# The choice by eleven rounds of three bits, gathers a stage ahead and new order lists in a gated-attention and expert kernel

## The chip, the cores and the metric

The kernel runs on one core of one Trainium2 chip. The metric is device time in microseconds (us), the median of repeated runs. One more execution was recorded by the hardware profiler; its rows are what the prediction reads. The engines are TensorE (PE in the rows, PEld for its weight loads), VectorE (DVE), ScalarE (ACT), GpSimd (POOL) and SyncE (SP), which only issues transfers.

## What is computed

Four batches of 512 tokens with 512 features go through a gated cross-attention and then a gated mixture of experts. Cut to what matters:

```python
kv   = ctx @ W_k.T + b_k                          # 4 x 512 x 128
sim  = (layernorm(x) @ kv) @ kv.T * scale         # per batch, 512 x 512
attn = softmax(normalised(sim) * gamma + beta)
x    = x + tanh(g_xattn) * attn
h    = layernorm(x)                               # 2048 tokens
shared = ffn(h, shared_w1, shared_w2)             # x1 * silu(x2) @ w2
aff  = sigmoid(h @ gate_w + bias)                 # 7 experts
mask = top 2 experts of each token
sel[e] = the 292 tokens with the largest affinity among those that chose e
routed[sel[e]] += ffn(h[sel[e]], w1[e], w2[e]) * aff
out  = x + tanh(g_ffn) * (shared + routed)
```

The 292nd largest affinity of each expert must be found exactly, and ties are filled in token order.

## The kernel before, in words

It is written by hand: each engine has one list of calls, and semaphores order them between engines. An engine works strictly in its list's order, so where a call stands decides what it can hold up.

*Front.* For batch b TensorE transposes the context (`context`), projects keys (`keys`), transposes x (`x_cols`, four columns) and the centred keys (`keys_back`), multiplies (`attend`, `scores`). ScalarE copies each result out of PSUM (`context_copy`, `x_copy`, `keys_copy`, `keys_back_copy`, `out_copy`) and sums squares (`squares`, `exps`, `row_squares`). VectorE computes row statistics of x (`x_stats`), centres keys, scales scores by an inverse root that GpSimd computes (`score_variance`, `scale_scores`), adds the attention (`add_attention`) and normalises rows (`row_variance`, a root on GpSimd, `row_normal`). The rows are transposed again (`rows_back`) and split into two parts of reduced precision: ScalarE makes the upper (`rows_upper`), VectorE the lower (`rows_lower`); each product is three matmuls over such parts. Weights are split the same way (`upper_*`, `lower_w1`, `lower_w2`).

*Shared expert and gate.* `gate` and `logits` make the seven scores of each token, `take_logits` stores them. `up(f, half, part)` is 12 matmuls of 512 columns, `down(f, t)` 6. Between them `gate_tanh`, `gate_first`, `gate_second`, `gate_upper` and `gate_lower` form the hidden values. A down tile is added to x in two ways: tiles below `EARLY` = 10 are scaled by ScalarE (`shared_rows`) and added to the output in DRAM by accumulating transfers that GpSimd issues (`add_to_out`), while x itself was stored before; the rest are added by VectorE (`add_shared`) and stored by SP (`store_sums`).

*Choice.* `choose_two` (from L1320, its first operation is the sign shift) marks each token's two experts and turns scores into ordered integers, cut into four byte planes masked by the choice (L1332). Eight rounds then find each expert's threshold, four bits at a time: `compare(r)` compares all scores of a plane with 15 candidates (four operations of 7 x 15 x 4 = 420 elements, L1353), `count(r)` sums them over partitions on TensorE (four matmuls of 420 columns, L451), `take_digit(r)` (L1358 to L1363) turns the sums into the next digit. Shared products stand between the counts on TensorE and gate steps between the rounds on VectorE. Then `flag`, `total_and_prefix`, `slots_of_chosen`, `place_told`, `hot_slots`, `slot_products` and `token_rows` give each expert's list of token rows `tok`.

*Routed experts.* GpSimd gathers 292 rows for an expert in three indirect transfers (`gather`, L1158) and adds its results to the output by three scattering ones (L1183). TensorE transposes the gathered rows of the next expert (`gathered`) inside the current expert's products; the first matmuls of an expert are on L712. Gathered rows lie in two buffers, so the gather of expert e + 2 waits until e's rows are transposed and its weights copied; in GpSimd's list it stands just ahead of the scatter of expert e, and behind that of e - 1.

The few lines of the choice that carry the size of a round:

```python
LEVELS, NIBBLE = 4, 16
CAND = NIBBLE - 1
ROUNDS = 2 * LEVELS
for q in range(NB):   # compare
    v.tensor_tensor(hit[:, q, :, :, :], bc(scores[:, :, ts].unsqueeze(2), [P, E, CAND, TT]),
                    bc(thresholds[:, :, :].unsqueeze(1), [P, E, CAND, TT]), ALU.is_ge)
```

## Time and profile before

| | |
|---|---|
| median of 3 runs | 260.25 us (259.28 to 262.13) |
| profiled execution | 259.54 us |
| its span | 257.8 us |
| granted TensorE clock, mean | 0.973 |
| busy share PE, DVE, ACT, POOL | 89%, 71%, 54%, 32% |
| bytes moved | 38.19 MB, mean 148 GB/s |

The page cuts the span into 40 slices of 6.4 us and prints each engine's busy share in tenths, the clock that TensorE was granted and the transfers' load:

```profile
PE   2998968999999988999999996999979999999920
PEld 1745533677568766677668775978868989898810
DVE  0486989789979898888988999858473848482300
ACT  3447995797794854221334304565745666664320
POOL 6502002003021020100112257315757858553370
PEclk9999995999999999999999999999999999999995
DMA  6899000800436023910750939994979988370651
```

Slices 1 to 16 are the front, 17 to 23 the choice, 25 to 38 the seven routed experts. An instruction's duration in the rows includes the time in the pipeline, so two of one kind start closer together than one lasts.

### The profile page before, as it was taken

The numbers are of one execution on the slowest core, as the hardware profiler recorded it, in microseconds if no ns is written. First come the engines' busy times: TensorE is split into PE (matmuls) and PEld (weight loads), VectorE is DVE, ScalarE is ACT, GpSimd is POOL, SyncE is SP. The second block draws the span as 40 slices with busy tenths as digits, with TensorE's granted clock in tenths as the row PEclk, the third lists the DMA queues.
The fourth block names the chain that finished last, engine by engine and source line by source line (L and its number), as shares of the span: only waits on it lengthen the run. The fifth ranks groups of instructions, "written<-read, shape, count | busy, mean of one in ns | idle before, by whom it ended". The sixth has DMA issues, their size and how long they took to land.

```text
span 257.8 us, 3584 instructions
## 1 busy us (share of the span) xinstructions
PE 228.6 (89%) x1182; PEld 173.4 (67%) x1182; DVE 183.9 (71%) x458; ACT 138.9 (54%) x314; POOL 82.8 (32%) x88
## 2 busy tenths in 40 slices
PE   2998968999999988999999996999979999999920
PEld 1745533677568766677668775978868989898810
DVE  0486989789979898888988999858473848482300
ACT  3447995797794854221334304565745666664320
POOL 6502002003021020100112257315757858553370
PEclk9999995999999999999999999999999999999995
DMA  6899000800436023910750939994979988370651
GB/s 208 279 350 317 5 0 17 309 0 0 185 143 245 0 93 119 385 57 3 89 74 12 165 82 335 233 377 98 238 213 226 249 280 161 96 95 5 89 68 25
DMA packets 23084, 38.19 MB, mean 148 GB/s; under 512 B 4054, under 2 KB 6262, under 8 KB 23066
## 3 DMA queue, kind: packets, MB, share of 16 engines
q1 hardware_dynamic: 16570, 25.30, 28.5%
q0 software_dynamic: 5536, 11.62, 25.3%
q10 hardware_dynamic: 960, 1.05, 1.2%
q8 instruction: 9, 0.15, 0.2%
q14 instruction: 9, 0.07, 0.1%
HBM read 22.70 MB, written 15.26 MB: 147 GB/s over the span
## 4 chain that ended last, share of the span: by engine, by line
PE 40%; DVE 21%; ACT 12%; issue 11%; DMA 7%; POOL 4%; DVEq 2%; POOLq 1%; ACTq 0%
PE bank L375 22%; PE bank L370 6%; PE bank L408 4%; DMA out<-yr,tok_out 3%; DMA xg_tail<-h_rows,tok 2%; ACT junk L849 2%; POOL out L1183 2%; DVEq L1194 2%; DVE hit L1353 2%; DVE prob L1228 2%; DVE prob L1222 2%; ACT yr L1032 2%; DVE xs L1239 2%; PE bank L451 1%; PE bank L426 1%
## 5 line engine op out<-in xcount | busy, mean ns | idle before, releaser
L1183 POOL DMA_INDIRECT out<-yr,tok_out x21 | 34.2, 1629 | 31.6 <-ACT yr L1032 16.4
L784 ACT ACTIVATE gT_hi<-gf 128x292 fp32r<-128x292 f32 (+3 forms) x23 | 11.4, 500 | 30.2 <-DVE gf L1275 18.0
L375 PE MATMUL bank<-hT_hi,w1s_hi 128*128 128x512 f32 x64 | 26.7, 417 | 0.3 <-DVE th L1270 0.3
L375 PE MATMUL bank<-hT_hi,w1s_lo 128*128 128x512 f32 x64 | 25.1, 392 | 0.0
L375 PE MATMUL bank<-hT_lo,w1s_hi 128*128 128x512 f32 x64 | 25.0, 390 | 0.0
L1032 ACT ACTIVATE yr<-bank,wslot 128x512 f32<-128x512 f32 (+1 forms) x21 | 13.9, 687 | 13.5 <-PE bank L375 12.6
L375 PE MATMUL bank<-w2s_hi,gT_hi 128*128 128x512 f32 (+1 forms) x50 | 20.8, 415 | 0.0
L375 PE MATMUL bank<-w2s_hi,gT_lo 128*128 128x512 f32 (+1 forms) x50 | 19.6, 392 | 0.0
L375 PE MATMUL bank<-w2s_lo,gT_hi 128*128 128x512 f32 (+1 forms) x50 | 19.5, 391 | 0.0
L1158 POOL DMA_INDIRECT xg<-h_rows,tok x14 | 15.6, 1114 | 12.2 <-issue 7.7
L1109 POOL TENSOR_TENSOR rs<-vs,mhalf 128x4 f32<-128x4 f32 x4 | 4.5, 1114 | 45.1 <-DVE vs L1215 45.1
L408 PE MATMUL bank<-xT,kvc 128*128 128x512 f32 x32 | 17.5, 699 | 1.6 <-ACT xT L784 1.3
L1291 DVE TENSOR_TENSOR w1r_lo<-w_raw,w1r_hi 128x512 fp32r<-128x512 f32 x16 | 10.8, 690 | 10.5 <-ACT w1r_hi L784 10.2
L784 ACT ACTIVATE hgT_hi<-bank 128x292 fp32r<-128x292 f32 x28 | 10.5, 408 | 13.0 <-PE bank L370 12.0
L1291 DVE TENSOR_TENSOR w1s_lo<-w_raw,w1s_hi 128x512 fp32r<-128x512 f32 x16 | 10.6, 687 | 7.4 <-ACT w1s_hi L784 7.2
L1128 POOL DMA_DIRECT2D out<-xs x5 | 6.3, 1266 | 29.3 <-ACT xs L875 29.3
L414 PE MATMUL bank<-kvcT,outT 128*128 128x512 f32 x32 | 14.6, 598 | 0.3 <-ACT outT L784 0.3
L375 PE MATMUL bank<-hgT_hi,w1r_hi 128*128 128x292 f32 x48 | 14.5, 303 | 0.0
L375 PE MATMUL bank<-hgT_hi,w1r_lo 128*128 128x292 f32 x48 | 14.3, 297 | 0.0
L375 PE MATMUL bank<-hgT_lo,w1r_hi 128*128 128x292 f32 x48 | 14.2, 297 | 0.0
L375 PEld LDWEIGHTS bank<-hT_hi,w1s_hi 128*128 128x128 f32 x64 | 12.1, 189 | 3.1 <-DVE th L1270 0.7
L375 PEld LDWEIGHTS bank<-hT_hi,w1s_lo 128*128 128x128 f32 x64 | 12.0, 188 | 2.7
(221 smaller groups left out, 641.4 us busy)
## 6 DMA issues: line engine op xcount, KB each, us to landing
w_raw<-in_L_ffn_routed_w SPq DMA_DIRECT2D x7, 1024.0 KB
w_raw<-in_L_ffn_routed_w SPq DMA_DIRECT2D x7, 512.0 KB
xs<-in_x SPq DMA_DIRECT2D x3, 1024.0 KB, 12.1
h_rows<-h SPq DMA_DIRECT2D x3, 1024.0 KB, 4.2
out<-xs POOLq DMA_DIRECT2D x5, 512.0 KB
out<-xs SPq DMA_DIRECT2D x2, 1024.0 KB, 6.8
out<-xs SPq DMA_DIRECT2D x4, 512.0 KB, 5.5
ctxb<-in_ctx SPq DMA_DIRECT2D x4, 256.0 KB, 6.8
```

The lines of the kernel that those rows point to most:

```text
L370: return nc.tensor.transpose(out_ap, in_ap, ident[0:n, 0:n])
L375: last = nc.tensor.matmul(out_ap, w, m, start=first and n == 0, stop=final and n == len(todo) - 1)
L408: last = nc.tensor.matmul(front_bank(b, ATTEND)[:, :], kvc[:, j, :], xT[:, j, :], start=j == 0, stop=j == TT - 1)
L414: nc.tensor.matmul(bank[t][:, :], outT[:, t * P:(t + 1) * P], kvcT[:, :], start=True, stop=True).then_inc(p_S, 1)
L784: return nc.scalar.activation(dst, src, ACT.Copy)
L849: nc.scalar.activation(junk[:, t, :], tile_of(at), ACT.Square, bias=nmean[:, at:at + 1], accum_out=ssx[:, at:at + 1]).then_inc(e_ssx, 1)
L1032: nc.scalar.activation(yr[e % 2][0:GSZ[g], g, :], down_bank(e, g)[0:GSZ[g], :], ACT.Copy, scale=w).then_inc(f_y, 1)
L1128: g_.dma_start(out_rows[f, :, 2 * half:2 * half + 2, :], xs[:, at:at + 2, :], accum_op=ALU.add).then_inc(st_y, 16)
L1158: g_.indirect_dma_start(gathered_rows(e, g)[0:GSZ[g], 0:HW], None, h_dram, index(tok, e, g), bounds_check=T).then_inc(gath[e % 2][g], 16)
L1183: g_.indirect_dma_start(rows, index(tok_out, e, g), yr[e % 2][0:GSZ[g], g, :], None, bounds_check=T - 1, compute_op=ALU.add).then_inc(scat ...
L1194: return v.drain()
L1291: v.tensor_tensor(w[1][:, k, :], raw[:, k, :], w[0][:, k, :].bitcast(F32), ALU.subtract).then_inc(w1_lo, 1)
```

## The change

The choice takes digits of three bits: each score's ordered integer is read in six levels of six bits (`LEVELS`), cut out by shift and mask (`level_bits`) when a level begins, each level in two rounds, but one round for the last two bits. That makes eleven rounds. A round has 7 candidates, and a comparison covers half of the tokens: two operations of 7 x 7 x 8 = 392 elements, and four count matmuls of 196 columns. The upper part of a number is masked by `keep` instead of a product with `mask`.

`EARLY` goes from 10 to 14: tiles (2, 2) to (3, 1) are also scaled by ScalarE and added by accumulating transfers, two `add_to_out` more and two `store_sums` fewer, and `add_to_out(1, 1)` moves behind the first two gathers. `down(3, 3)` moves behind the first gathered transposes, its `add_shared` behind the first `gathered_lower`. The gather of expert e + 3 stands ahead of the scatter of expert e. Seven matmuls on a zeroed tile open TensorE's list. Loads of x and shared weights are issued in another order, `slots_ps` lies in bank 3, the banks of the front are assigned anew, and the lists of TensorE, ScalarE and VectorE for front and choice are written anew. The core of the diff:

```diff
-LEVELS = 4
-NIBBLE = 16
-CAND = NIBBLE - 1
-ROUNDS = 2 * LEVELS
-EARLY = 10
+BITS = 6
+LEVELS = -(-32 // BITS)
+DIGIT = 8
+CAND = DIGIT - 1
+HT = NT // 2
+ROUNDS = 2 * LEVELS - 1
+WARM = 7
+EARLY = 14
...
             load_x(1)
-            load_x(2)
-            load_raw(0, sw1[0], sw2[0])
             sp.wait_ge(p_ctxT, 1)
             load_ctx(2)
+            load_x(2)
             load_x(3)
+            sp.wait_ge(p_ctxT, 2)
+            load_ctx(3)
+            load_raw(0, sw1[0], sw2[0])
...
-                    pe.wait_ge(r_hit, NB * r + q + 1)
-                    last = nc.tensor.matmul(counts, ones[:, :], hit[:, q, :, :, :].rearrange("p e c t -> p (e c t)"),
+                    if q % 2 == 0:
+                        pe.wait_ge(r_hit, 2 * r + q // 2 + 1)
+                    last = nc.tensor.matmul(counts, ones[:, :], hit[:, q // 2, :, :, q % 2 * TT:q % 2 * TT + TT].rearrange("p e c t -> p (e c) t"),
                                             start=q == 0, stop=q == NB - 1)
...
+            pe.wait_ge(c_warm, 1)
+            for _ in range(WARM):
+                nc.tensor.matmul(bank[0][:, :], junk[:, 0, 0:P], junk[:, 0, :], start=True, stop=True)
             pe.wait_ge(c_pool, 2)
-            context(0)
             pe.wait_ge(ld_wk, 16)
             transpose(bank[7][:, 0:C], Wk_rows[:, :]).then_inc(c_wk, 1)
...
             pe.wait_ge(c_start, 3)
@@ -617,56 +626,56 @@
             pe.wait_ge(e_hT, 14)
             up(2, 1, 0)
             count(1)
-            down(0, 1)
             pe.wait_ge(e_hT, 15)
-            down(0, 2)
+            up(2, 1, 1)
             count(2)
             pe.wait_ge(e_hT, 16)
+            down(0, 2)
+            count(3)
+            pe.wait_ge(e_y, 1)
+            up(3, 0, 0)
+            count(4)
+            pe.wait_ge(e_y, 2)
             down(0, 3)
+            count(5)
             pe.wait_ge(e_u, 5)
             down(1, 0)
-            count(3)
-            pe.wait_ge(e_y, 1)
-            up(2, 1, 1)
-            count(4)
             pe.wait_ge(e_g, 5)
-            up(3, 0, 0)
-            count(5)
+            down(1, 1)
+            count(6)
             pe.wait_ge(e_u, 6)
-            down(1, 1)
-            pe.wait_ge(e_y, 2)
             down(1, 2)
-            count(6)
+            count(7)
+            pe.wait_ge(e_g, 6)
+            up(3, 0, 1)
+            count(8)
             pe.wait_ge(e_y, 3)
-            up(3, 0, 1)
-            count(7)
+            down(1, 3)
+            count(9)
+            pe.wait_ge(e_u, 7)
+            up(3, 1, 0)
+            count(10)
             pe.wait_ge(e_y, 4)
-            down(1, 3)
-            pe.wait_ge(e_y, 5)
             down(2, 0)
             pe.wait_ge(c_start, 4)
             total_and_prefix()
-            pe.wait_ge(e_g, 6)
+            pe.wait_ge(e_y, 5)
             down(2, 1)
-            pe.wait_ge(e_u, 7)
-            up(3, 1, 0)
             pe.wait_ge(e_y, 6)
+            down(2, 2)
+            pe.wait_ge(e_y, 7)
             up(3, 1, 1)
-            pe.wait_ge(e_y, 7)
+            pe.wait_ge(e_g, 7)
+            down(2, 3)
+            pe.wait_ge(e_y, 8)
             slot_products(0)
-            pe.wait_ge(e_g, 7)
-            down(2, 2)
             slot_products(1)
-            pe.wait_ge(e_y, 8)
-            down(2, 3)
+            pe.wait_ge(e_u, 8)
+            down(3, 0)
             pe.wait_ge(e_y, 9)
-            down(3, 0)
+            down(3, 1)
             pe.wait_ge(e_y, 10)
-            down(3, 1)
-            pe.wait_ge(e_u, 8)
...
+            pe.wait_ge(e_y, 11)
+            pe.wait_ge(e_g, 8)
+            pe.wait_ge(e_y, 12)
+            pe.wait_ge(r_idx, 1)
             gathered_first()
+            down(3, 3)
+
...
             gather(0)
             gather(1)
+            add_to_out(1, 1)
             add_to_out(2, 0)
+            add_to_out(2, 1)
+            add_to_out(3, 0)
+            def gather_into_free(e):
+                pool.wait_ge(q_hgT, KD * (e - 1))
+                pool.wait_ge(f_w, e - 1)
+                gather(e)
+
+            gather_into_free(2)
             for e in range(E):
-                if e + 2 < E:
-
-                    pool.wait_ge(q_hgT, KD * e + KD)
-                    pool.wait_ge(f_w, e + 1)
-                    gather(e + 2)
+                if e + 3 < E:
+                    gather_into_free(e + 3)
...
+                v.scalar_tensor_tensor(keep[:, :, :], one[:, 0, :, :], -1.0, one[:, 1, :, :], ALU.mult, ALU.subtract).then_inc(r_one, 1)
+                settle()
+                v.tensor_tensor(ordered[:, :, :], ordered[:, :, :], keep[:, :, :], ALU.bitwise_and)
+                settle()
+                level_bits(0)
+                settle()
+                v.tensor_copy(top[:, :, :], bits[:, :, :])
+                settle()
+
+            def level_bits(level):
+                low_bit = max(32 - BITS * (level + 1), 0)
+                width = 32 - BITS * level - low_bit
+                v.tensor_scalar(bits[:, :, :], ordered[:, :, :], low_bit, 2 ** width - 1, ALU.logical_shift_right, ALU.bitwise_and)
+
+            def high_digit(r):
+                return r % 2 == 0 and r < ROUNDS - 1
 
             def compare(r):
                 level = r // 2
-                scores, thresholds = rest, low if r % 2 else high
+                scores, thresholds = rest, high if high_digit(r) else low
                 if r % 2:
-                    above = plane[:, LEVELS - 1, :, :] if level == 0 else rest[:, :, :]
+                    above = top[:, :, :] if level == 0 else rest[:, :, :]
                     v.tensor_tensor(rest[:, :, :], above, per_expert(digit[:, :]), ALU.subtract)
                     settle()
                 elif level > 0:
                     v.tensor_tensor(above_by[:, :, :], rest[:, :, :], per_expert(digit[:, :]), ALU.subtract)
                     settle()
-                    v.scalar_tensor_tensor(rest[:, :, :], above_by[:, :, :], 512.0, plane[:, LEVELS - 1 - level, :, :], ALU.mult, ALU.add)
+                    v.scalar_tensor_tensor(rest[:, :, :], above_by[:, :, :], 512.0, bits[:, :, :], ALU.mult, ALU.add)
                     settle()
                 else:
-                    scores = plane[:, LEVELS - 1, :, :]
-                for q in range(NB):
-                    ts = slice(q * TT, (q + 1) * TT)
-                    v.tensor_tensor(hit[:, q, :, :, :], bc(scores[:, :, ts].unsqueeze(2), [P, E, CAND, TT]),
-                                    bc(thresholds[:, :, :].unsqueeze(1), [P, E, CAND, TT]), ALU.is_ge).then_inc(r_hit, 1)
+                    scores = top
+                for half in range(2):
+                    ts = slice(half * HT, (half + 1) * HT)
+                    v.tensor_tensor(hit[:, half, :, :, :], bc(scores[:, :, ts].unsqueeze(2), [P, E, CAND, HT]),
+                                    bc(thresholds[:, :, :].unsqueeze(1), [P, E, CAND, HT]), ALU.is_ge).then_inc(r_hit, 1)
+                if r % 2 and level + 1 < LEVELS:
+                    level_bits(level + 1)
...
             x_stats(0)
             x_stats(1)
-            x_stats(2)
             score_variance(0)
-            lower_w1(SHARED, (0,))
             centre_keys(1)
             dve.wait_ge(ld_gb, 32)
             scale_scores(0)
             negative_logits(0)
+            x_stats(2)
             x_stats(3)
             dve.wait_ge(c_iota, 7)
...
             centre_keys(2)
             score_variance(1)
+            add_attention(0)
+            scale_scores(1)
             row_variance(0)
-            scale_scores(1)
+            negative_logits(1)
             row_normal(0)
-            lower_w1(SHARED, (1,))
-            negative_logits(1)
-            lower_w1(SHARED, (2,))
+            lower_w1(SHARED, (0, 1, 2))
+            rows_lower(0, (0,))
+            centre_keys(3)
+            lower_w1(SHARED, (3,))
+            rows_lower(0, (1,))
+            add_attention(1)
+            score_variance(2)
+            rows_lower(0, (2, 3))
+            scale_scores(2)
+            row_variance(1)
+            negative_logits(2)
+            gate_first(0, 0)
+            row_normal(1)
             dve.wait_ge(c_gw, 2)
             v.tensor_tensor(gw[:, :, LO:LO + E], gw_raw[:, :, LO:LO + E], gw[:, :, 0:E].bitcast(F32), ALU.subtract).then_inc(c_gw, 1)
-            rows_lower(0, (0,))
-            lower_w1(SHARED, (3,))
-            rows_lower(0, (1, 2, 3))
-            lower_w2(SHARED, (0,))
-            add_attention(1)
-            score_variance(2)
+            add_attention(2)
+            gate_second(0, 0)
+            rows_lower(1, (0,))
+            score_variance(3)
+            rows_lower(1, (1,))
+            gate_first(0, 1)
+            scale_scores(3)
             dve.wait_ge(ld_eb, 16)
             take_logits(0)
-            gate_first(0, 0)
-            scale_scores(2)
-            row_variance(1)
-            centre_keys(3)
-            negative_logits(2)
-            row_normal(1)
-            gate_second(0, 0)
-            gate_first(0, 1)
-            add_attention(2)
+            rows_lower(1, (2,))
             row_variance(2)
-            rows_lower(1, (0, 1, 2))
+            rows_lower(1, (3,))
+            negative_logits(3)
             row_normal(2)
-            score_variance(3)
-            rows_lower(1, (3,))
             gate_second(0, 1)
-            scale_scores(3)
+            take_logits(1)
+            gate_lower(0, 0)
+            gate_first(1, 0)
             rows_lower(2, (0,))
-            negative_logits(3)
-            take_logits(1)
+            add_attention(3)
             rows_lower(2, (1,))
-            add_attention(3)
-            gate_first(1, 0)
+            gate_second(1, 0)
+            lower_w2(SHARED, (0,))
+            rows_lower(2, (2,))
             row_variance(3)
-            gate_lower(0, 0)
-            gate_second(1, 0)
+            rows_lower(2, (3,))
+            lower_w2(SHARED, (1,))
             row_normal(3)
-            rows_lower(2, (2, 3))
             gate_first(1, 1)
             gate_lower(0, 1)
-            rows_lower(3, (0, 1))
+            rows_lower(3, (0, 1, 2, 3))
+            take_logits(2)
+            gate_second(1, 1)
             gate_lower(1, 0)
-            rows_lower(3, (2, 3))
-            lower_w2(SHARED, (1,))
-            gate_second(1, 1)
-            take_logits(2)
             take_logits(3)
             settle()
             choose_two()
             compare(0)
-            gate_lower(1, 1)
+            gate_first(2, 0)
             take_digit(0)
+            gate_second(2, 0)
             compare(1)
-            gate_first(2, 0)
+            lower_w1(0, (0,))
             take_digit(1)
             compare(2)
             gate_first(2, 1)
             take_digit(2)
             compare(3)
-            gate_second(2, 0)
+            gate_lower(1, 1)
             take_digit(3)
             compare(4)
-            gate_lower(2, 0)
             take_digit(4)
             compare(5)
             gate_second(2, 1)
@@ -1521,32 +1567,31 @@
             compare(6)
             take_digit(6)
             compare(7)
+            gate_first(3, 0)
+            take_digit(7)
+            compare(8)
+            take_digit(8)
+            compare(9)
+            gate_lower(2, 0)
+            take_digit(9)
+            compare(10)
             gate_lower(2, 1)
-            take_digit(7)
+            take_digit(10)
             flag()
-            gate_first(3, 0)
             gate_second(3, 0)
             slots_of_chosen()
             place_told()
             hot_slots(0)
+            hot_slots(1)
+            token_rows()
             gate_first(3, 1)
-            hot_slots(1)
             gate_second(3, 1)
-            token_rows()
             gate_lower(3, 0)
+            lower_w1(0, (1,))
             gate_lower(3, 1)
-            lower_w1(0, (0,))
-            add_shared(2, 2)
-            add_shared(2, 3)
-            lower_w1(0, (1,))
-            add_shared(3, 0)
-            lower_w1(0, (2,))
-            add_shared(3, 1)
+            lower_w2(0, (0, 1))
+            lower_w1(0, (2, 3))
             add_shared(3, 2)
...
             for k in range(KD):
                 gathered_lower(0, k)
+            add_shared(3, 3)
             lower_w1(1, range(W1N))
```

## Rows read from the trace of the kernel before

**Rows 1.** Busy us by stage: PE, PEld, DVE, ACT, POOL; clock, DMA share, GB/s

```profile
24.29:102.39 78.10, 72.54 (x324) 49.61 (x322) 68.47 (x158) 58.59 (x145) 8.31 (x11) 0.96 0.26 93
102.39:136.90 34.51, 34.11 (x151) 24.36 (x150) 30.01 (x88) 9.13 (x18) 3.60 (x4) 1.00 0.49 121
149.39:159.44 10.05, 7.97 (x41) 6.03 (x39) 9.86 (x18) 1.77 (x6) 7.42 (x7) 1.00 0.68 204
159.44:247.00 87.56, 84.55 (x535) 73.22 (x535) 52.79 (x129) 51.56 (x111) 47.78 (x35) 1.00 0.75 181
```

**Rows 2.** Timeline of TensorE in the front: start us, us, engine, line, operation

```profile
8.67 3.52 PE L370 MATMUL bank<-ident,xs 128*128 128x128 f32 x16
25.77 3.60 PE L408 MATMUL bank<-xT,kvc 128*128 128x512 f32 x8
40.06 6.68 PE L408 MATMUL bank<-xT,kvc 128*128 128x512 f32 x8 [1.26 <-ACT xT L784]
47.02 1.91 PE L370 MATMUL bank<-ident,h 128*128 128x128 f32 x16
```

**Rows 3.** Waits, whole span: who waited for whom, us in total, times, longest

```profile
PE bank L370 <- DMA ctxb<-in_ctx: 4.6, 1, 4.6
DVE vh L1244 <- ACT junk L849: 2.9, 3, 1.5
```

**Rows 4.** Timeline of VectorE from `x_stats(2)` to the first `scale_scores`

```profile
17.74 2.47 DVE L1199 BATCH_NORM_STATS2 bnx<-xs 128x6 f32<-128x512 f32 x4 [0.64 <-DMA xs<-in_x]
24.29 1.41 DVE L1222 SCALAR_TENSOR_TENSOR prob<-bank,rs,gamma_b 128x512 f32<-128x512 f32 x2 [0.44 <-POOL rs L1109]
```

**Rows 5.** Busy time by stage, columns as in Rows 1, two us of `attend(2)`

```profile
42.00:44.00 2.00, 2.00 (x4) 0.94 (x3) 2.00 (x6) 0.01 (x1) 0.00 (x0) 0.50 0.00 0
```

**Rows 6.** A round with no other operation, from VectorE's timeline and the chain

```profile
128.45 0.59 DVE L1358 TENSOR_REDUCE csum<-bank 128x105 f32<-128x420 f32 x1
129.74 0.28 DVE L1345 TENSOR_TENSOR above_by<-rest,digit 128x112 bf16<-128x112 bf16 x1
130.44 1.24 DVE L1353 TENSOR_TENSOR hit<-rest,high 128x420 bf16<-128x420 bf16 x4
132.13 0.60 DVE L1358 TENSOR_REDUCE csum<-bank 128x105 f32<-128x420 f32 x1 [0.45 <-PE bank L451]
...
127.50 0.73 PE bank L451 x4
128.23 2.76 PE bank L375 x12
```

**Rows 7.** Groups by line of VectorE: line, operation, shapes, count, busy us, mean ns

```profile
L1572 DVE TENSOR_TENSOR hgT_lo<-bank,hgT_hi 128x292 fp32r<-128x292 f32 x28 | 12.0, 455 | 1.6 <-ACT hgT_hi L784 1.6
L1259 DVE TENSOR_TENSOR hT_lo<-bank,hT_hi 128x512 fp32r<-128x512 f32 x16 | 10.6, 686 | 2.0 <-ACT hT_hi L784 2.0
L1332 DVE TENSOR_TENSOR plane<-ordered,mask 128x448 bf16<-128x448 uint8 x1 | 0.8, 850 | 0.1
```

**Rows 8.** Timelines of VectorE and TensorE from the choice's start to the gathered rows

```profile
102.39 0.22 DVE L1320 TENSOR_SCALAR signs<-z 128x112 int32<-128x112 int32 x1
136.90 0.28 DVE L1367 TENSOR_TENSOR flags<-rest,digit 128x112 bf16<-128x112 bf16 x1
155.90 0.75 DVE L1284 SCALAR_TENSOR_TENSOR xs<-bank,gt,xs 128x512 f32<-128x512 f32 x1 [0.19 <-issue]
...
156.75 1.06 PE L370 MATMUL bank<-ident,xg 128*128 128x128 f32 x8 [0.89 <-issue]
```

**Rows 9.** Timeline of TensorE: first products of experts 2 and 3, a wait between

```profile
184.22 0.70 PE L712 MATMUL bank<-hgT_hi,w1r_hi 128*128 128x292 f32 x4
190.75 0.80 PE L370 MATMUL bank<-ident,xg 128*128 128x128 f32 x2 [1.51 <-DMA xg<-h_rows,tok]
198.42 0.70 PE L712 MATMUL bank<-hgT_hi,w1s_hi 128*128 128x292 f32 x4
```

**Rows 10.** Busy time by stage, columns as in Rows 1, behind the first gathers

```profile
158.00:164.00 6.00, 4.82 (x37) 4.61 (x36) 6.00 (x14) 5.13 (x12) 2.06 (x2) 1.00 1.04 248
```

321 lines of the change are left out of this document (162 added, 159 removed).

## The prediction

> **What bounds the kernel now.** I read the page's slices, then busy time by stage [rows 1], then the chain that ended last and the timelines where it changes hands. Three stages have different limits. From 24.3 to 102.4 us (attention, the shared expert's first products, the gate) VectorE is busy 68.5 of 78.1 us and TensorE 72.5, and there a busy TensorE is not always a fast one. From 102.4 to 136.9 (the choice) both are nearly full: 34.1 and 30.0 of 34.5. From 159.4 to 247 TensorE is busy 84.6 of 87.6, and most of what is missing are waits for gathered rows. Behind 247 only the last scatters land; nothing in the change shortens that, so I carry it over.
>
> The profiled execution took 259.5 us; its span is 257.8. The sum below is made against 257.8. The median of the three timed runs, 260.25, lies 2.45 above that span, and the final number adds this back.
>
> **Part 1: new lists in the front, with a warm-up.** Seven matmuls of zeros now run while the first inputs load. Before, sixteen x transposes near the start take 3.52 us and sixteen later ones 1.91 [rows 2]: TensorE then works at the lower of its two levels, 1.2 GHz, though the profile prints a granted clock of 1.00 there. The dummies are 512 columns wide; twelve products of that width take 2.76 us at full speed [rows 6], so seven at half speed are 3.2 us. They lie in the 4.6 us in which TensorE waited for its first input [rows 3], and cost nothing; without that cover they would cost their 3.2. If the clock has risen by the time x is there, the transposes save 1.6 us, and `keys_back(0)`, now ahead of x column 3, lets `attend(0)` start on its first copies. I count 2.0 us at the first score scaling: 22.3 instead of 24.29 [rows 4]. Bounds: 0.4 (one group of four transposes earlier, no faster clock) and 2.8 (the keys fast too).
>
> The Trainium skill (TensorE: Matmul & The Clock Gate, "What's actually happening") says the array starts cold at half its clock and is ungated by activity. The half speed of the first transposes agrees.
>
> Against that, the list moves `x_stats(2)`, before at 17.74 in time that VectorE had idle (2.47 us, 3.1 with its small steps), and one weight split behind the first scaling [rows 4]: 3.1 + 0.6 = 3.7 us more in the bounded stretch. VectorE's work from the scaling to the choice becomes 68.5 + 3.7 = 72.2 us.
>
> The rest is idle time, before 78.1 - 68.5 = 9.6 us, of which 2.9 is the wait for row squares [rows 3]. The new lists put work behind each wait: `add_attention(0)` covers GpSimd's root, `lower_w1` and `centre_keys(3)` stand between pieces of `rows_lower`, batch 3's attention moves ahead of the first `up`, two gate steps stand around `rows_lower(3, ...)`. I went through VectorE's new list by hand with the spacing of the same operations before (0.6 us for a subtraction of 512, 0.67 for a scaling, 0.46 for a normalisation) and asked at each wait when ScalarE and TensorE deliver. The longest waits left are 0.6 before `row_normal(3)`, 0.6 before `rows_lower(3, 0)` and 0.7 for `logits(3)`; the total is 3.8, and 4.4 with handoffs that I rounded away. So the choice starts at 22.3 + 72.2 + 4.4 = 98.9 instead of 102.39: **3.5 us gained**. Bounds: with all of the old idle time kept 104.1 (1.7 lost); with 2 us idle 96.5 (5.9 gained). One weak place stays: before, `attend(2)` takes 6.68 us where `attend(1)` takes 3.60 [rows 2], for after 3.9 us with one group of transposes the granted clock is 0.50 [rows 5]. By the new list TensorE still waits there for the same centred keys, so I expect this dip again, 2 us earlier, and nothing gained at it.
>
> **Part 2: eleven rounds of three bits.** A round before with no other operation in it [rows 6]: sum, threshold and digit 1.29 us (128.45 to 129.74), two steps to the next plane 0.70, four comparisons and the wait for the counts 1.69 (130.44 to 132.13), in all 3.68. By size: from 292 to 512 elements a subtraction goes from 455 to 686 ns, 1.05 ns an element [rows 7]. The sum reads 196 elements instead of 420, threshold and digit 49 instead of 105: 0.23 + 0.06 + 0.06 less, 0.94. Two comparisons of 392 replace four of 420: half of 1.24, and 0.42 until the counts are back. A round is then 2.69 us, or 2.34 where one step precedes it. The fixed part dominates: VectorE alone needs some 28 us for eleven rounds, as for eight before.
>
> The Trainium skill (VectorE: DVE Perf Modes, "Mode 2×_1P — pack two bf16 into one 32-bit read") asks for 16-bit data at unit step for the doubled rate. Four comparisons of 420 in 1.24 us are 0.74 ns an element with all fixed cost, below the 1.05 of f32: the rows agree, and the new inner run of 8 has unit step too.
>
> `level_bits` is one shift-and-mask of 112 elements, 0.22 us like the sign shift [rows 8], behind the comparisons while TensorE counts; its cover gone it would cost 1.1 us over five. `keep`, mask, level 0 and `top` take 0.35 + 0.35 + 0.29 + 0.29 where a 0.35 mask and the 0.85 us plane were [rows 7]: nothing changes. TensorE's count costs 0.73 us for 4 x 420 columns [rows 6]; by columns the new one is 0.34, with weights loaded each time I take 0.4. Between counts stands a 12-matmul product (2.76 us) in six of ten gaps, a 6-matmul one (1.38) in four. A long gap is 2.76 + 0.4 = 3.15; a short one takes what VectorE needs, 2.5 to 2.9. With the nine operations put into the rounds the flags come 36.4 us after the choice starts, before 136.90 - 102.39 = 34.5 [rows 8]: **1.9 lost**.
>
> From the flags (136.90) to the token rows (149.39) it was 12.5 us [rows 1, 8]. `gate_first(3, 0)` moves ahead, and two gate steps between and behind the hot slots move behind the token rows (3 x 0.6), TensorE being there in time: 10.7, **1.8 gained**. From the token rows to the first expert's product it was 10.05 us (149.39 to 159.44, [rows 1]). The transposes began at 156.75, right behind `add_shared(3, 3)` (155.90 + 0.75), which they waited for [rows 8]. That wait goes. Late instead is `gate_lower(3, 1)`: five VectorE steps behind the token rows, 3.2 us, then three down tiles of 1.38, 7.3 in all, then the transposes and ScalarE's copies as before. The last down tile fills TensorE's wait for these copies. 9.45 instead of 10.05: **0.6 gained**. Part 2 together: **0.5 gained**. Bounds: 2.5 gained, if the gathers land early without two stores beside them; 2 lost, if each round takes 0.2 longer.
>
> **Part 3: gathers a stage ahead.** Two expert starts, 184.22 and 198.42, lie 14.2 us apart, while the last periods are 12.4; the 14.2 holds 1.51 us of waiting for expert 3's rows [rows 9], which POOL issued behind expert 0's scatter, and slow first transposes after it. The new order issues them as soon as expert 1's rows are transposed, before that scatter. GpSimd's queue there holds four accumulating writes and one gather more than the scatters; the writes, 1.3 us each, end just before `gather(2)` could start anyway. Gain 1.8. `add_shared(3, 3)` stands in VectorE's list behind the first gathered rows and delays the next `hgT_lo`, 0.4 on TensorE. In the DMA queues 1 MB of stores goes and three accumulating writes of 0.5 MB come, into 158 to 164 us, where DMA is full at 248 GB/s [rows 10]: 6 us of it. Expert 2's weights queue behind them, needed by ScalarE some 8 us later, by TensorE 20. I count 0.2, bound 1.5. **1.2 gained** (0.5 lost to 2.3 gained).
>
> **Sum:** -3.5 - 0.5 - 1.2 = -5.2, so 252.6 for the span and 255.0 for the median.
>
> **Rivals.**
> A: the clock dips behind the choice. While VectorE does its five steps TensorE has small slot products and then nothing for some 3 us. A stretch of that kind ended at half clock before [rows 2, 5]. Four down tiles and the first product would run at half speed, 3.5 us lost: 258.5. Against it: half a down tile breaks the stretch. The Trainium skill (TensorE: Matmul & The Clock Gate, "HAM oscillation — how this bites in real kernels") says that gaps without matmuls put the array back to half clock; the clock row at 42 us agrees.
> B: the front's list does not fill VectorE. Idle time stays near 7.9 us, the moved statistics eat the rest, Part 1 gives 0: 258.5.
> C, slower: a round costs by its instructions, not its size: 3.68 and 3.33 us [rows 6] instead of 2.69 and 2.34. The four short gaps are then 1.0 longer each, the six long ones, now VectorE's too, 0.5, and the last digit 0.4: 7.4 more, 262.4. It ends above the old time from 0.75 us a round more than I count. Against it stands the slope of [rows 7].
> D: the warm-up works in full and no dip comes at 40 us; `attend(2)` gets its 3 us back: 252.0.
>
> **How the numbers follow.** Forecast 0.48, A 0.16, B 0.13, C 0.09, D 0.14. About 1% (2.6 us) is what a measurement of this kernel tells from no change. Below 257.65 lie most of the forecast, D, and small parts of A and B: 0.66. Within 1% lie most of A and B and the forecast's upper end: 0.23. Slower are C, and A with B together: 0.11. The range goes from D's lower end, 249.5, to A or B with the DMA bound, 260.5; outside are C and the ends of D.
>
> **What would show it.** The sign shift at about 99; x transposes in half the time; flags 36.4 us later, token rows 10.7 after them, the first expert product 9.45 after these; no wait for `xg`, periods of 12.0 to 12.8. The forecast is wrong if VectorE idles over 7 us between scaling and choice, if the granted clock falls after 100 us, or if a round without other work takes over 3 us.

## The result and the profile after

The changed kernel takes 262.89 us, the median of 16 executions (261.38 to 266.63). The kernel before, run beside it, has a median of 260.86 us over 16 (256.55 to 262.27). The ratio is 1.013, with a 95% interval of 1.0089 to 1.0171: the change makes the kernel slower by about 1%, where 255.0 us, 2% faster, was forecast. The ratio compares the means of the executions that lie within 1.5% of their kernel's fastest (7 of the 16 before, 14 of the 16 after); all sixteen against all sixteen give 1.010. The profiled execution took 262.56 us with a span of 260.8.

Busy time of each engine between the marks of [rows 1], in the changed kernel: first score scaling to choice, choice to flags, flags to token rows, token rows to the first expert product. The last three numbers are the granted TensorE clock, the DMA share and GB/s.

```profile
core 0: us, PE busy (x) PEld busy (x) DVE busy (x) ACT busy (x) POOL busy (x), PEclk, DMA share, GB/s
21.28:99.01 77.73, 71.62 (x322) 48.87 (x323) 71.72 (x168) 59.51 (x145) 8.91 (x11) 1.00 0.36 126
99.01:136.14 37.13, 35.31 (x174) 25.84 (x172) 30.05 (x102) 11.12 (x22) 4.39 (x5) 1.00 0.51 122
136.14:146.82 10.68, 9.79 (x66) 7.30 (x64) 9.40 (x33) 3.22 (x6) 1.00 (x2) 1.00 0.01 2
146.82:158.48 11.66, 9.53 (x37) 7.64 (x37) 7.33 (x14) 4.69 (x10) 9.03 (x9) 0.71 0.39 105
```

Set against the same marks of before, from the two profiled executions (start of a stretch to its end; negative is time gained):

| stretch | before, us | after, us | difference | forecast |
|---|---|---|---|---|
| start to the choice | 102.39 | 99.01 | -3.38 | -3.5 |
| choice to token rows | 47.00 | 47.81 | +0.81 | +0.1 |
| token rows to first expert product | 10.05 | 11.66 | +1.61 | -0.6 |
| first to last expert's first product | 76.23 | 79.52 | +3.29 | -1.2 |
| last expert's first product to the end | 22.13 | 22.80 | +0.67 | 0 |
| span | 257.8 | 260.8 | +3.0 | -5.2 |

So the first stretch behaves as forecast in this execution, the second loses 0.7 us more than that, and two turn round. First the clock. TensorE's timeline from the last slot product on (start, duration, idle time before), and the stretch by windows:

```profile
148.95 0.77 PE L378 MATMUL bank<-w2s_hi,gT_hi 128*128 128x512 f32 x1 [2.62 <-DVE gT_lo L1313]
150.37 0.63 PE L378 MATMUL bank<-w2s_hi,gT_hi 128*128 128x512 f32 x1
155.07 0.39 PE L378 MATMUL bank<-w2s_hi,gT_hi 128*128 128x512 f32 x1
```

```profile
148.00:150.00 2.00, 1.05 (x3) 0.83 (x3) 2.00 (x5) 1.77 (x3) 1.69 (x2) 0.50 0.16 23
152.00:154.00 2.00, 2.00 (x6) 1.54 (x5) 0.41 (x1) 0.64 (x1) 1.70 (x2) 0.50 0.40 133
154.00:156.00 2.00, 2.00 (x10) 1.56 (x10) 0.03 (x1) 0.69 (x1) 1.39 (x3) 0.86 0.51 133
```

TensorE waits 2.62 us for `gate_lower(3, 0)`. The granted clock falls to 0.50, which is 1.2 GHz, and the products of the down tiles start 0.43 us apart instead of 0.23 until 154.5. Some thirteen of them, 0.2 us each, are 2.6 us lost; TensorE counts as "busy" throughout. This is rival A.

Then the experts. First products of experts 1 and 2 in TensorE's timeline, a stage of 17.4 us where it was 12.8 before (and expert 2's stage is 12.4 where it was 14.2 [rows 9]):

```profile
171.01 0.38 PE L724 MATMUL bank<-hgT_hi,w1s_hi 128*128 128x292 f32 x1
188.41 0.70 PE L724 MATMUL bank<-hgT_hi,w1r_hi 128*128 128x292 f32 x4
```

TensorE in the long stage and in the same stage of before (busy time by window), then two of its waits in the long stage, then the clock between them:

```profile
171.01:188.41 17.40, 14.45 (x81) 12.26 (x80) 8.34 (x21) 8.15 (x19) 7.75 (x6) 0.90 1.05 291
171.46:184.22 12.76, 12.26 (x80) 10.73 (x80) 8.26 (x21) 8.12 (x19) 6.35 (x5) 1.00 0.73 169
177.63 0.33 PE L373 MATMUL bank<-ident,xg 128*128 128x128 f32 x1 [0.80 <-DMA xg<-h_rows,tok]
183.53 0.44 PE L373 MATMUL bank<-ident,xg 128*128 128x128 f32 x2 [1.48 <-DVE hgT_lo L1617]
180.00:182.00 2.00, 2.00 (x9) 1.74 (x8) 1.76 (x4) 0.63 (x1) 1.36 (x1) 0.53 1.04 363
```

So the 4.6 us have two parts. TensorE stands still for 2.95 us where it was 0.50: 1.47 in three waits for expert 2's gathered rows (one is shown) and 1.48 behind expert 2's weights. And it is busy for 2.2 us more with the same products, at a granted clock that falls to 0.53 behind the waits for rows.

The chain that ended last, in order of time, says what the last of these waits goes back to: one transfer of expert 2's weights, issued at 160.67 and landed 19.7 us later.

```profile
160.67 19.70 DMA w_raw<-in_L_ffn_routed_w
180.40 0.64 ACT w2r_hi L800
```

And what stood in the queues with it: GpSimd's four accumulating writes, and the first of ScalarE's waits for the same weights (timelines of GpSimd, then ScalarE).

```profile
156.63 5.09 POOL L1157 DMA_DIRECT2D out<-xs  x4
176.25 1.15 ACT L800 ACTIVATE w1r_hi<-w_raw 128x512 fp32r<-128x512 f32 x2 [4.33 <-DMA w_raw<-in_L_ffn_routed_w]
```

DMA throughput from 156 to 181 in 40 slices of 0.625 us: the engines are full from 160 on, but until 173.5 at 134 to 279 GB/s, and only then at 266 to 417.

```profile
GB/s 113 253 143 37 85 111 197 203 190 180 134 249 259 265 269 259 239 256 252 269 252 279 265 262 265 256 265 259 329 387 417 413 390 281 351 398 317 303 266 374
```

The wait for expert 3's rows [rows 9] is gone, as the third part said. In its place expert 2's rows and weights are late, one stage earlier, and cost three times as much.

### The profile page after: what moved, and what is told of

Its sections match the earlier page's. It is cut to its first block, busy times and chain, and to the rows that moved or that the text cites. A ratio compares the mean times of both kernels' runs of the same rounds, so it can differ in the third digit from the quotient of the medians.

```text
span 260.8 us, 3652 instructions
## 1 busy us (share of the span) xinstructions
PE 230.7 (88%) x1201; PEld 173.7 (67%) x1201; DVE 179.0 (69%) x465; ACT 141.7 (54%) x318; POOL 86.6 (33%) x91
## 3 DMA queue, kind: packets, MB, share of 16 engines
q10 hardware_dynamic: 960, 1.05, 1.2%
## 4 chain that ended last, share of the span: by engine, by line
PE 51%; DVE 19%; DMA 12%; ACT 7%; issue 4%; DVEq 2%; SPq 1%; POOL 1%; POOLq 0%
PE bank L378 32%; DMA w_raw<-in_L_ffn_routed_w 8%; PE bank L373 6%; DMA xs<-in_x 4%; PE bank L429 3%; PE bank L411 3%; PE bank L417 2%; DVEq L1228 2%; PE bank L455 2%; PE bank L724 2%; ACT square L852 2%; DVE w1s_lo L1325 1%; DVE hgT_lo L1617 1%; DMA Wk_rows<-in_L_xattn_W_k 1%; DVE prob L1256 1%
## 5 line engine op out<-in xcount | busy, mean ns | idle before, releaser
L800 ACT ACTIVATE gT_hi<-gf 128x292 fp32r<-128x292 f32 (+3 forms) x23 | 11.4, 497 | 30.9 <-DVE gf L1631 12.4
L378 PE MATMUL bank<-w2s_hi,gT_hi 128*128 128x512 f32 (+1 forms) x50 | 21.9, 438 | 2.6 <-DVE gT_lo L1313 2.6
L1059 ACT ACTIVATE yr<-bank,wslot 128x512 f32<-128x512 f32 (+1 forms) x21 | 13.9, 687 | 13.0 <-PE bank L378 12.1
L1325 DVE TENSOR_TENSOR w1r_lo<-w_raw,w1r_hi 128x512 fp32r<-128x512 f32 x16 | 10.7, 688 | 14.6 <-ACT w1r_hi L800 14.3
L378 PE MATMUL bank<-w2s_hi,gT_lo 128*128 128x512 f32 (+1 forms) x50 | 20.6, 412 | 0.0
L378 PE MATMUL bank<-w2s_lo,gT_hi 128*128 128x512 f32 (+1 forms) x50 | 20.5, 410 | 0.0
L411 PE MATMUL bank<-xT,kvc 128*128 128x512 f32 x32 | 15.1, 607 | 1.8 <-ACT xT L800 1.5
L1157 POOL DMA_DIRECT2D out<-xs x7 | 8.8, 1697 | 17.4 <-ACT xs L891 17.4
L378 PE MATMUL bank<-hgT_lo,w1r_hi 128*128 128x292 f32 x48 | 14.2, 296 | 0.0
L373 PE MATMUL bank<-ident,xg 128*128 128x128 f32 x56 | 10.6, 289 | 3.9 <-DVE hgT_lo L1617 2.4
## 6 DMA issues: line engine op xcount, KB each, us to landing
xs<-in_x SPq DMA_DIRECT2D x3, 1024.0 KB, 13.5
```

Of the source, the lines that this page charges most:

```text
L373: return nc.tensor.transpose(out_ap, in_ap, ident[0:n, 0:n])
L378: last = nc.tensor.matmul(out_ap, w, m, start=first and n == 0, stop=final and n == len(todo) - 1)
L411: last = nc.tensor.matmul(front_bank(b, ATTEND)[:, :], kvc[:, j, :], xT[:, j, :], start=j == 0, stop=j == TT - 1)
L800: return nc.scalar.activation(dst, src, ACT.Copy)
L1059: nc.scalar.activation(yr[e % 2][0:GSZ[g], g, :], down_bank(e, g)[0:GSZ[g], :], ACT.Copy, scale=w).then_inc(f_y, 1)
L1157: g_.dma_start(out_rows[f, :, 2 * half:2 * half + 2, :], xs[:, at:at + 2, :], accum_op=ALU.add).then_inc(st_y, 16)
```

## The experiments

Two questions: what makes expert 2's weights and rows late (T1, the accumulating writes that `EARLY = 14` adds; T2, the gathers a stage ahead), and what the clock, the front list and the rounds are each worth. "Unread matmuls" are bf16 products of 512 columns into a free bank that nothing reads; the output stays the same. Kernels of one group ran on one chip beside the same executions of the kernel before. The groups ran on different chips, so that kernels of two groups are compared by their ratios. The starts and stages below are those of each kernel's one profiled execution.

### First group: the clock, the gathers, the writes

**Unread matmuls in the wait before `down(3, 0)`**

```diff
+FILL = 11
...
             slot_products(1)
+            for _ in range(FILL):
+                nc.tensor.matmul(bank[7][:, :], ones[:, :], iota_s[:, :, :].rearrange("p s t -> p (s t)"), start=True, stop=True)
             pe.wait_ge(e_u, 8)
             down(3, 0)
```

> The changed kernel with eleven matmuls of 512 bf16 columns, whose results nobody reads, between the second half of slot_products and down(3,0). Theory 1 (the clock fell because TensorE waited 2.6 us for gT while VectorE made slots and token rows): the granted clock of 148 to 156 stays at 1.00, the twelve matmuls of a down tile are again 0.23 us apart, the first expert product comes 2.5 to 3 us earlier, 260 instead of 262.6 us in all; unless the weights of expert 2 are still what expert 1 waits for, and then only a part of it arrives at the end. Rival (the clock fell for what came before, or the matmuls of down themselves are too sparse for it): the clock falls to 0.5 all the same and the time does not move. Second rival: the 2.9 us are regained before expert 0 and all given back in expert 1's stage, because the weights land at a time of their own: the first product at 155.6, the time within 0.5 us of the changed kernel.

262.76 us, ratio to before 1.0113 [1.0063, 1.0163]. The clock stays at full:

```profile
148.00:150.00 2.00, 1.82 (x9) 0.62 (x7) 1.91 (x4) 0.65 (x2) 0.96 (x1) 1.00 0.00 0
```

From the token rows to the first expert product it now takes 9.5 us instead of 11.7: 2.2 us back. But expert 1's stage grows to 21.6 us, and the whole is not faster. (The profiled execution took 265.19 us, 2.4 above the median, so the stage will be shorter in most.) In this chain it is not the weights but expert 2's gathered rows, issued behind the four writes, that end it:

```profile
164.72 17.74 DMA xg<-h_rows,tok
```

So the second rival of this run holds: the times are the same within 0.2 us, and what is gained ahead of the late transfers is waited away.

**Gathers in their old place**

```diff
-            gather_into_free(2)
             for e in range(E):
-                if e + 3 < E:
-                    gather_into_free(e + 3)
+                if e + 2 < E:
+                    gather_into_free(e + 2)
```

> The changed kernel with the gathers of expert e+2 issued in expert e's stage again, as in the kernel before; everything else as changed. Theory T2 (the gather of expert 3, put into 169 to 173, makes expert 2's weights late): the weights land by about 176, expert 1's stage falls from 17.4 to about 13 us, and expert 2's stage grows by the gather wait of 1.5 us; 259.5 us in all. Theory T1 (the four accumulating writes do it): the weights still take some 18 us and more, expert 1's stage stays over 16.5 us, and the wait for the gather comes on top or hides behind them: 262.5 to 264 us.

267.45 us, ratio 1.0288 [1.0155, 1.042]. Expert 1's stage is 19.0 us. T2 falls: ScalarE waits 4.59 us for the weights (4.33 in the changed kernel) and TensorE 2.6 for expert 2's rows, without the gather of expert 3 among them. Expert 3's stage takes 0.9 us more than in the changed kernel, waiting for rows; the rest of what this kernel's profiled execution is longer comes from its front, where the choice starts at 102.66 (third group).

**The four writes behind expert 3's gather**

```diff
             gather(1)
-            add_to_out(1, 1)
-            add_to_out(2, 0)
-            add_to_out(2, 1)
-            add_to_out(3, 0)
...
                     gather_into_free(e + 3)
+                if e == 0:
+                    add_to_out(1, 1)
+                    add_to_out(2, 0)
+                    add_to_out(2, 1)
+                    add_to_out(3, 0)
```

> The changed kernel with the four accumulating writes of the last tiles issued behind the gather of expert 3 instead of behind that of expert 1. Theory T1 (the accumulating writes of 156.6 to 161.7 take the DMA engines from expert 2's weights): the weights land 3 to 5 us earlier, expert 1's stage falls from 17.4 to about 13 us, 258.5 us in all. Theory T2 (the gathers do it): no change of the landing, 262.5 us. Rival: the writes now meet the weights of expert 3 or hold the first scatter, and the 4 us come back one stage later: expert 2's stage 16 us, 262 us in all.

266.88 us, ratio 1.0298 [1.0169, 1.0427], and the clearest reading of all. Expert 1's stage is 12.7 us: T1 holds. Its throughput in the slices of 156 to 181, where the writes begin only at 173:

```profile
GB/s 107 233 177 57 0 0 0 170 347 285 213 157 380 396 347 361 383 410 410 393 415 394 386 404 385 283 322 412 346 157 92 108 210 206 206 193 177 200 131 170
```

From 163.5 to 173.5 the slices show 283 to 415 GB/s without the writes, and behind 174 they show 92 to 210 with them. (One short fall, to 157 at 162.9, has no accumulating write near it; I leave it open.) The price moved with them: expert 0's scatter needs the writes landed, and GpSimd issued it 12.7 us after it could have.

```profile
173.07 5.09 POOL L1157 DMA_DIRECT2D out<-xs  x4
190.85 1.66 POOL L1218 DMA_INDIRECT out<-yr,tok_out  x1 [12.70 <-issue]
```

ScalarE then waits 9.3 us until it may write `yr` again, and expert 3's stage becomes 21.9 us. The rival named there came, one stage later than I had put it.

**Unread matmuls and late writes together**

> Both edits together: the eleven matmuls and the four writes behind the gather of expert 3. If the clock and the writes are the two causes (2.9 and 4 us): 255.5 us, below the kernel before. If the weights are late for another reason, the filled wait shows nothing at the end: 261 to 262 us.

266.11 us, ratio 1.0243 [1.0125, 1.036]. Neither number came: the clock holds (9.6 us from token rows to the first product), expert 1's stage is 12.7, and expert 3's is 20.7 for the same late scatter. Two causes removed and one new wait put in.

### Second group: fewer or earlier writes

**`EARLY` at 10 again.** The tiles 10 to 13 are added by VectorE and stored whole, as before; writes (1, 1) and (2, 0) stay behind the gathers.

```diff
-EARLY = 14
+EARLY = 10
...
+            store_sums(2, 1)
+            store_sums(3, 0)
             store_sums(3, 1)
...
+            add_shared(2, 2)
+            add_shared(2, 3)
             lower_w1(0, (2, 3))
+            add_shared(3, 0)
+            add_shared(3, 1)
             add_shared(3, 2)
```

> The changed kernel with EARLY at 10 again: the tiles 10 to 13 are added by VectorE and stored whole instead of being written accumulating; two accumulating writes are left behind the gathers of experts 0 and 1, and two plain stores of 0.5 MB stand beside them. Theory T1 (what is slow is the accumulating write, about 4.5 us of the DMA engines for each of 0.5 MB, since four of them took 18 us in the run where they stood alone with expert 3's weights): expert 1's stage falls from 17.4 to 12.5 to 13.5 us, no later stage stalls, 258.5 us in all. Rival (it is the bytes, not their kind): two plain stores bring the same 1 MB, so the stage stays at 16 us and over, 262 us. The 2.8 us that VectorE works more in 152 to 156 lie in its idle time there.

260.87 us, ratio 0.9963 [0.9921, 1.0005]. Expert 1's stage is 13.9 us, a little above the 12.5 to 13.5 of T1, and the stages behind it are 12.4. One weight transfer still holds ScalarE a little:

```profile
175.29 1.15 ACT L802 ACTIVATE w1r_hi<-w_raw 128x512 fp32r<-128x512 f32 x2 [1.06 <-DMA w_raw<-in_L_ffn_routed_w]
```

The same bytes went out in plain stores, issued from 154.7 on where the writes began at 156.6, so it is the kind of the transfer and not its size. What in the kind costs is open: every accumulating write here is issued by GpSimd and every plain store of these tiles by SyncE, and no run tells the adding from the issuing queue.

**Two of the four writes before the gathers**

```diff
             add_to_out(1, 0)
+            add_to_out(1, 1)
+            add_to_out(2, 0)
             pool.wait_ge(p_x1, 2 * NB)
...
             gather(1)
-            add_to_out(1, 1)
-            add_to_out(2, 0)
             add_to_out(2, 1)
```

> The changed kernel with the first two of the four accumulating writes issued before the gathers, from about 136 and 139 on, where the DMA engines carry nothing; the other two stay. Theory T1: as much as two such writes cost, 9 us of the DMA engines, leaves the stretch of the weights, which land by 173 to 175: expert 1's stage 12.5 to 13.5 us, 258.5 us in all. Rival (the weights are late for the last writes alone, or the early ones now hold the gathers of expert 0): the first product moves from 158.5 to 160 and more, or the stage stays above 16 us; 262 us and more.

258.78 us, ratio 0.9934 [0.9899, 0.997]. Expert 1's stage is 12.8 us. GpSimd's timeline, and a window that holds those two writes and nothing else:

```profile
137.90 1.20 POOL L1157 DMA_DIRECT2D out<-xs  x1 [11.08 <-ACT xs L891]
140.59 1.20 POOL L1157 DMA_DIRECT2D out<-xs  x1 [1.49 <-ACT xs L891]
137.00:146.00 9.00, 8.79 (x51) 6.65 (x49) 8.15 (x28) 3.43 (x7) 3.39 (x4) 1.00 0.73 117
```

This is the price that the prediction lacked. 117 GB/s over 9 us is 1.05 MB, the two writes, and they kept all sixteen DMA engines busy for 0.73 x 9 = 6.6 us: 3.3 us for each 0.5 MB. Plain stores of 2.1 MB run alone in the changed kernel from 47 to 52.6, in 40 slices of 46 to 56:

```profile
GB/s 0 0 0 0 156 385 385 369 311 385 385 377 385 385 385 385 385 385 385 377 385 410 385 377 385 385 238 0 0 0 0 0 0 0 0 0 0 0 0 0
```

They keep the engines busy for 5.7 us, which is 1.4 us for 0.5 MB; a load of weights at 400 GB/s takes 1.3.

**All of it: unread matmuls, `EARLY` at 10, both remaining writes before the gathers**

> Eleven unread matmuls in the wait before down(3,0), EARLY at 10, and both accumulating writes that are left issued before the gathers. If the clock's fall and the accumulating writes are the whole of what the changed kernel lost: first product 2.9 us earlier than in the changed kernel for the same start of the choice, all stages at 12.4 to 12.7 us, 255.5 us in all, 4 us faster than the kernel before. If something else is late once the weights are not (the gather of expert 2 or 3, the first scatter): one stage of 14 us and more remains, 258 us.

256.26 us, ratio 0.9841 [0.9799, 0.9883]. Stages 12.9, 12.8 and then 12.4; 9.5 us from the token rows (149.40) to the first product (158.88). Nothing else was late behind the weights. This kernel keeps the new front list, the eleven rounds and the gathers ahead.

**The kernel before with only the gathers ahead** (the loop of the changed kernel in GpSimd's list, nothing else)

> The kernel before with the gathers of expert e+3 ahead of the scatters of expert e as the only change. By the prediction's third part: the wait of 1.5 us for expert 3's gather goes, expert 2's stage falls from 14.2 to 12.5 us, the rest stays, 258.5 us. By what the changed kernel showed, if gathers a stage earlier collide with the weights: expert 1's stage grows from 12.8 by 1 us or more and eats the gain, 260 us.

257.37 us, ratio 0.9878 [0.9821, 0.9935]: some 3 us faster, with an interval of 1.7 to 4.7. The 2.1 us that the first theory gave lie inside it, the second theory's 0.6 do not. Its stages are 13.5 (the granted clock is 0.77 from 160 to 166), 12.7, and then 12.4. Expert 2's stage is 1.8 us shorter than before, as the third part said. (The profiled execution took 258.65 us and shows only 0.9 us of the gain in its span.) No transfer is late; one accumulating write stands behind its first gathers. So the useful part of the change was this one.

### Third group: the front and the rounds

**Nine unread matmuls in the two waits before `attend(2)`**, in the changed kernel and in the kernel before

```diff
             pe.wait_ge(e_kvT, 3)
+            pe.wait_ge(c_start, 3)
+            pe.wait_ge(c_iota, 7)
+            unread(7, 6)
             keys_back(2)
             pe.wait_ge(e_xT, 11)
+            unread(4, 3)
             attend(2)
```

> The changed kernel with nine unread matmuls of 512 bf16 columns in TensorE's two waits before attend(2) (six ahead of keys_back(2), three ahead of attend(2)). If the fall of the clock at 36 to 44 comes from these waits: it stays at 1.00 there, attend(2) takes 3.98 us in every execution, the choice starts at 99.0 to 99.5 and not at up to 102.7 as in some runs of the changed front, and the whole is 1 to 2 us faster than the changed kernel, 261.5 us. If it comes from what ran before (transposes), the choice starts at 100 to 102.7 as before, 262.9 us. The weights' stage of 17 us and more is in this kernel too.

> The kernel before with the same nine unread matmuls before attend(2). If the front list itself brought 3.5 us in the changed kernel, the choice starts here, with attend(2) at full clock, at 99.5 to 100.5 against 102.39 with the fall, and the changed front without a fall is still 0.5 to 1.5 us ahead (2 us of it the first twelve transposes at full clock). If the gain of the changed front was nothing but the absent fall, both start the choice at the same time, 99.0. In all 257.5 us against 260.6 if the fall costs 3 us here.

263.06 us (five executions) and 259.97 us (four), beside 261.37 of the kernel before, whose seven executions lie between 256.57 and 263.54; no interval was worked out in this group, and the whole times decide nothing. Neither kernel shows a fall of the clock between 34 and 46. The kernel before, where `attend(2)` took 6.68 us [rows 2]:

```profile
41.12 3.60 PE L408 MATMUL bank<-xT,kvc 128*128 128x512 f32 x8
```

And VectorE's first instruction of the choice, the changed front and then the old one:

```profile
99.27 0.22 DVE L1362 TENSOR_SCALAR signs<-z 128x112 int32<-128x112 int32 x1
100.32 0.22 DVE L1328 TENSOR_SCALAR signs<-z 128x112 int32<-128x112 int32 x1
```

With the fall absent from both, the new list with its warm-up is 1.05 us ahead, not 3.4. As a whole, the old kernel kept little of its earlier choice: with nothing done about its gathers, the stages of experts 2 and 3 became 13.8 and 15.9 us. In the second of them TensorE waits 1.7 us for rows, and the granted clock is 0.50 from 204 to 206 behind these waits. In the changed kernel with the nine, expert 1's stage is 20.2 us.

**No warm-up**

```diff
-WARM = 7
+WARM = 0
```

> The changed kernel without the seven warm-up matmuls. By the prediction's first part they bring the first transposes to full speed: without them the first twelve take 3.5 us again instead of 1.53, the first scaling starts 2 us later (24.3), and the choice 2 us later (101) if no fall of the clock comes in between. If the front waits for loads instead, nothing moves: choice at 99.

264.60 us. TensorE's keys and first x transposes, without the warm-up:

```profile
6.93 2.05 PE L394 MATMUL bank<-ctxT,WkT 128*128 128x512 f32 x2 [0.78 <-ACT ctxT L800]
8.77 2.27 PE L373 MATMUL bank<-ident,xs 128*128 128x128 f32 x12
```

With it, in the profiled execution of the changed kernel:

```profile
6.00 1.10 PE L394 MATMUL bank<-ctxT,WkT 128*128 128x512 f32 x2 [0.78 <-ACT ctxT L800]
7.28 1.53 PE L373 MATMUL bank<-ident,xs 128*128 128x128 f32 x12 [0.18 <-DMA xs<-in_x]
```

The choice starts at 101.21 without it and at 99.01 with it. The 2.2 us are what was expected, but not all of them are the warm-up's: the first scaling starts at 22.94 without it and at 21.28 with it, 1.7 us instead of 2, and in the kernel without it the clock also fell to 0.50 at 38:40, which the expectation had left out of its 2 us. And the warm-up does its work only in some executions. Of eleven profiled executions with exactly these seven matmuls, four show the Wk transposes and keys at full speed (choice at 98.6 to 99.3), two the keys (100.1), and five neither, as here in the next kernel (choice at 101.2 to 102.7):

```profile
6.79 2.05 PE L392 MATMUL bank<-ctxT,WkT 128*128 128x512 f32 x2 [0.78 <-ACT ctxT L794]
```

The five start the first scaling at 22.7 to 23.1 and so look like the kernel without a warm-up. The seven of the second and third kind also show a clock of 0.50 to 0.53 at 38:40, and the four of the first kind no fall (one of the four has the unread matmuls there). The Trainium skill (TensorE: Matmul & The Clock Gate, "What's actually happening") says that the start-up at half clock is "run-variable"; these rows agree.

**Eight rounds of four bits in the changed kernel** (thresholds, planes and counts of before; the other lists as they are, with the products and gate steps of the last three gaps moved into earlier ones)

> The changed kernel with the choice in eight rounds of four bits again (byte planes, fifteen thresholds, counts of 420 columns). From the rows of both kernels: choice start to flags 37.1 us with eleven rounds, 34.5 with eight in the old list. By the cost of the instructions (a round 3.68 us for four bits against 2.69 and 2.34 for three) the flags come 2 to 2.6 us earlier here, everything else stays, and the changed kernel gets 2 us faster, 260.8 us. Rival: the interval is set by TensorE's products between the counts and not by the rounds; then the flags come at the same 37 us and nothing moves.

264.63 us. The flags come 36.3 us after the choice starts, 0.8 less than with eleven rounds and not 2 to 2.6. And the token rows come 12.6 us after the flags instead of 10.7, since TensorE was behind: two products stand between the last count and the total where there was one, and VectorE waited.

```profile
140.50 0.62 DVE L1404 TENSOR_TENSOR_SCAN cum<-nofirst,bank 128x224 f32<-128x224 f32 x1 [1.79 <-PE bank L460]
```

### Fourth group: what was still open

**Eight rounds, and `down(2, 0)` behind the total**

```diff
             count(7)
             pe.wait_ge(e_u, 7)
             up(3, 1, 0)
-            pe.wait_ge(e_y, 4)
-            down(2, 0)
             pe.wait_ge(c_start, 4)
             total_and_prefix()
+            pe.wait_ge(e_y, 4)
+            down(2, 0)
```

(The diff is against the kernel just above.)

> The changed kernel with eight rounds of four bits, as in the run before, but with down(2,0) behind the total instead of ahead of it, so that TensorE meets the flags when they are there. There the rounds ended 0.8 us earlier and the flags then waited 1.79 us for TensorE. If only the order was to blame: choice start to flags 36.3 us, flags to token rows 10.7 us, together 47.0 against 47.63 with eleven rounds, and the kernel 0.6 us faster than the changed one. Rival (between the choice and the first product TensorE's products set the time, and a shorter choice only moves its idle time): token rows earlier by 0.6 us, the first expert product not, because down(3,0) and what is behind it wait for TensorE.

262.98 us, ratio 1.0075 [1.0041, 1.011]; the interval overlaps that of the changed kernel. Choice to token rows takes 48.0 us, against 47.8 with eleven rounds; choice to first product 59.6 us, against 59.5. Also with the order mended, fewer rounds bring nothing to the first product.

**The best combination with the front's waits filled** (the nine unread matmuls and two more ahead of `keys(0)`), with eleven rounds and with eight; and **the kernel before with the gathers ahead and the nine unread matmuls**

> The combination that was fastest so far (unread matmuls before down(3,0), EARLY at 10, both accumulating writes before the gathers; 256.3 us) with the nine unread matmuls before attend(2) and two more of them ahead of keys(0). If the falls of the clock in the front are what is left of the difference between its executions: the choice starts at 99.3 to 100.3 in place of 101.5, the span is 254 to 255, the time 254.5 us. If the fall at 38 is not stopped where the warm-up came too late: choice at 101 to 102 as before, 256.3 us.

> The same combination as the second of these four, with eight rounds of four bits and down(2,0) behind the total. If a shorter choice reaches the first expert product: 0.5 us faster than with eleven rounds, 254.0 us. If TensorE's products set that stretch: the same within 0.3 us.

> The kernel before with only the gathers ahead and the nine unread matmuls before attend(2): neither the front's new list nor the eleven rounds nor EARLY at 14. The two alone gave 257.4 us (gathers ahead) and a choice start 2 us earlier (unread matmuls). If they add up: 255.5 to 256 us, as fast as the combination built on the changed kernel, and the new front list, the rounds and EARLY are worth nothing. If the changed list is worth 1 us: 256.5 to 257 us against 254.5.

255.84 us, ratio 0.9809 [0.9756, 0.9862], with eleven rounds; 255.81 us, 0.9798 [0.9745, 0.985], with eight; 255.08 us, 0.978 [0.9726, 0.9833], for the kernel before with two small edits. Its choice and token rows, and those of the first of the three:

```profile
100.02 0.22 DVE L1331 TENSOR_SCALAR signs<-z 128x112 int32<-128x112 int32 x1
146.88 0.18 DVE L1431 SCALAR_TENSOR_TENSOR tok<-slots 128x21 int32<-128x21 f32 x1
```

```profile
99.16 0.22 DVE L1363 TENSOR_SCALAR signs<-z 128x112 int32<-128x112 int32 x1
146.96 0.18 DVE L1474 SCALAR_TENSOR_TENSOR tok<-slots 128x21 int32<-128x21 f32 x1
```

The new front is 0.9 us ahead at the choice, and by the token rows the two stand together. From the choice to the first expert product it takes 57.45 us with eleven rounds, 57.50 with eight in the new lists, and 57.08 in the old ones. No difference between the three whole times can be told. The two edits to the kernel before make it 2.2% faster (interval 1.7% to 2.7%), and all the rest of the change adds nothing that can be told.

| kernel | first product | stages of experts 0, 1, 2, 3 | time, us |
|---|---|---|---|
| before | 159.44 | 12.0, 12.8, 14.2, 12.5 | 260.86 |
| after | 158.48 | 12.5, 17.4, 12.4, 12.4 | 262.89 |
| after, gathers in their old place | 161.38 | 12.6, 19.0, 12.5, 13.3 | 267.45 |
| after, writes behind expert 3's gather | 158.63 | 12.5, 12.7, 12.4, 21.9 | 266.88 |
| after, two writes before the gathers | 159.91 | 12.6, 12.8, 12.4, 12.4 | 258.78 |
| after, all mended, front filled | 156.61 | 12.9, 12.8, 12.4, 12.4 | 255.84 |
| before, gathers ahead | 158.84 | 13.5, 12.7, 12.4, 12.4 | 257.37 |
| before, gathers ahead, front filled | 157.10 | 12.1, 12.7, 12.4, 12.4 | 255.08 |

The times of this table come from several chips, on which the kernel before has 259.94 to 260.92 us.

## Why the prediction was wrong

The forecast was -5.2 us in the span, the profiled execution has +3.0. Of the 8.2 us between them 4.5 lie in the experts' stages, 2.2 between token rows and first product, 0.7 between choice and token rows, 0.7 in the tail and 0.1 in the front.

**The step that failed is the DMA term of Part 3.** "I count 0.2, bound 1.5": it was 4.6 us (17.4 against 12.8), three times the bound. The row was there: [rows 10] shows the engines full at 248 GB/s with one accumulating write among the traffic, and I read "full" as a fact about bytes. An accumulating write takes 3.3 us of all engines for 0.5 MB where a plain store takes 1.4, so by an estimate from these two prices three more of them in place of two plain stores are 3 x 3.3 - 2 x 1.4 = 7.1 us more of queue ahead of the weights. The weights were issued at 160, some 11 us before expert 1's first product, and needed within 1 us of it; expert 2's rows were late with them, though the third part expected no wait for `xg`. TensorE stood still for 2.5 us more, and the clock that fell in these waits cost another 2.2. This is shown by moving the writes (stage 12.7 or 12.8) against moving the gathers (19.0).

**Rival A came, with 0.16.** The prediction had its wait (3 us; 2.62 measured) and its price (3.5; some 2.6 by the rows, of which 2.2 came back when the wait was filled), and set against it that half a down tile breaks the stretch. It does not come in between: `down(3, 0)` itself waits for `gate_lower(3, 0)`. Part 2's 0.6 gained between the token rows and the first product was 1.6 lost, and Part 2 as a whole lost 2.4, beyond its bound of 2; with the wait filled the stretch takes 9.5 to 9.6 us, as forecast (9.45).

**Part 1: the number right, by luck.** 98.9 was forecast for the choice, 99.01 measured. The first scaling starts at 21.28, 3.0 us earlier than before where I counted 2.0 and bounded it by 2.8: the list alone gives 1.35 (22.94 without the warm-up), the warm-up 1.66. VectorE then has 71.7 us of work (72.2 forecast) and 6.0 idle (4.4), halfway to rival B's 7.9. These errors, -1.0, -0.5 and +1.6, cancel. Besides, I expected the clock's fall at `attend(2)` to come again with nothing gained, and it was absent: `attend(2)` took 3.98 us. About 2.1 of the 3.4 us gained are that fall (102.39 against 100.32 in the old list), 1.05 the list and the warm-up together. So the condition of rival D came in this execution, and its 3 us on top of the forecast did not. In seven of eleven profiled executions of this front the fall did come, and the choice started at 100.1 to 102.7, 1.2 to 3.8 later than forecast for that very case. A single profiled execution of either kernel is therefore no measure of the front: the old front has 102.39 in the kernel before and, with a shorter fall, 101.06 in the one with only the gathers ahead.

**Part 2: the sizes held, but they decide nothing.** Rounds in VectorE's timeline of the changed kernel, one of the short gaps, then TensorE's count:

```profile
129.54 0.36 DVE L1403 TENSOR_REDUCE csum<-bank 128x49 f32<-128x196 f32 x1 [0.68 <-PE bank L455]
130.53 0.28 DVE L1385 TENSOR_TENSOR rest<-rest,digit 128x112 bf16<-128x112 bf16 x1
130.88 0.63 DVE L1396 TENSOR_TENSOR hit<-rest,low 128x392 bf16<-128x392 bf16 x2
132.16 0.35 DVE L1403 TENSOR_REDUCE csum<-bank 128x49 f32<-128x196 f32 x1
131.29 0.62 PE L455 MATMUL bank<-hit,ones 128*128 128x196 bf16 x4 [0.38 <-DVE hit L1396]
```

Sum, threshold and digit take 0.99 us (0.94 forecast), two comparisons 0.63 (0.62), a short round 2.62 with a gate step in it; the count takes 0.62 (0.52 in the rounds beside it) where I took 0.4, near the 0.73 us of the old one in spite of less than half the columns. Flags after 37.1 (36.4), token rows 10.7 after them (10.7). Rival C, a round costed by its instructions, is out. The prediction had noted that TensorE was nearly full in the choice, and made no use of it: it is busy 35.3 of 37.1 and 9.8 of 10.7 us there. With eight rounds or eleven it has the same products to do before the first expert, and the runs agree that a shorter choice moves its idle time only; none of them took a product away to prove it.

**Part 3's gain was there.** I counted 1.8 for the gathers, and against the profiled kernel before (76.23 us from first to last expert) they bring 1.9 in the kernel before with the front filled (74.32). With the old gathers the filled front has 79.23: there they are worth 4.9 us, since expert 4's rows are late too and the clock falls behind the wait.

**The tail** lost 0.67 us, which I had carried over. Across the kernels here it lies between 21.9 and 22.8; I leave it open.

## What to carry to other kernels

Price a transfer by the time it keeps the DMA engines, read in a window where it runs alone, and not by its bytes. A write that accumulates costs 2.3 plain stores here, and belongs where the engines are idle (136 to 146 in this kernel). Before costing an edit by its own instructions, ask which engine has work left until the next joint mark: here the rounds and the front list together moved the token rows by nothing and the first product by 0.5 us (156.61 against 157.10). Look also at what a wait does to the clock: the wait of 2.62 us on TensorE cost its length and then 2.6 us in slow products. Filling it with products that nobody reads was a cheap test of that and also the repair.

## What the runs showed of the hardware that was not expected

- A 0.5 MB accumulating write to memory, issued by GpSimd: 3.3 us of sixteen engines, some 160 GB/s, against 385 GB/s of plain stores by SyncE and up to 417 of weight loads in the same kernels.
- A warm-up of 3.15 us, always at the same place, raised TensorE's clock before the first keys in six of eleven profiled executions and too late in five. (This is read from durations, 1.10 us against 2.05 for the two keys products; the profile prints a granted clock of 1.00 in both.) In the four executions where the transpose of W_k was fast too the clock did not fall again at 38 us, in the seven others it did; why the two go together is open. Nine unread matmuls kept the clock up there in all five kernels that had them, also in those without a warm-up.
- TensorE's clock fell to half in 2.62 us without products from 146.3 on, and stayed there until 154.5 with the engine fully busy from 148.95 on.
- With the memory queues full, SyncE's own issue of one 0.5 MB load took 5.20 us instead of 0.5, and nothing behind it in its list can start meanwhile (here the next load was not due before 184.5):

```profile
163.73 5.20 SPq L320 DMA_DIRECT2D w_raw<-in_L_ffn_routed_w  x1
```
